# Layer norms of two expert stages move from VectorE to GpSimd, and their router is rebuilt on a padded MAX8 and a match-replace

## The reference

```
n = (t - mean(t)) / sqrt(var(t) + 1e-5)
p = softmax(n @ router)             # 8 experts
top2 values and indices of p
block 0: cw = the two values / their sum, at their experts, else 0; out = t + n + sum_e cw[e] * ffn_e(n)
block 1: cw = the two values, at their experts, else 0;             out = t + sum_e cw[e] * ffn_e(n)
```

## Time and profile before

| what | value |
|---|---|
| median of 3 runs | 6992.14 us (6990.91 to 6999.84) |
| profiled execution, own time (its span) | 6996.9 us |
| TensorE matmul / weight load busy | 5469.8 us (78%) / 4119.1 us (59%) |
| VectorE busy | 6258.5 us (89%) |
| ScalarE busy | 3507.3 us (50%) |
| GpSimd busy | 4062.8 us (58%) |
| mean granted TensorE clock | 0.748 |

### The profile page before, as it was taken

How to read it: one execution, slowest core, us unless ns; L and a number is a source line. 1 busy time by engine, 2 the same in 40 slices (tenths; PEclk the granted TensorE clock), 3 DMA queues, 4 the chain that set the end, 5 groups by cost and what they waited for, 6 DMA issues and landing times. The chain is left out here.

```text
span 6996.9 us, 144425 instructions
## 1 busy us (share of the span) xinstructions
PE 5469.8 (78%) x30242; PEld 4119.1 (59%) x30242; DVE 6258.5 (89%) x25629; ACT 3507.3 (50%) x7250; POOL 4062.8 (58%) x2812
## 2 busy tenths in 40 slices
PE   4777788887878777887878787878878787777777
PEld 2665566565656565665656565656656565656654
DVE  3999999999989999999989999998999999999941
ACT  1344455555545455555545555554545555555543
POOL 2555656565656566565656566565656566656542
PEclk9667777777777787777777777777767777777777
DMA  2111111111111111111111111111111111111100
GB/s 56 28 30 33 29 29 32 30 33 31 33 30 33 27 33 29 32 31 30 33 30 33 27 34 29 35 28 30 33 30 33 30 30 26 28 27 28 30 15 13
DMA packets 501061, 212.34 MB, mean 30 GB/s; under 512 B 339456, under 2 KB 495744, under 8 KB 500096
## 3 DMA queue, kind: packets, MB, share of 16 engines
q1 hardware_dynamic: 500096, 201.91, 12.8%
HBM read 145.29 MB, written 56.37 MB: 29 GB/s over the span
## 5 line engine op out<-in xcount | busy, mean ns | idle before, releaser
L515 POOL TENSOR_SCALAR b_r<-b_r 128x1024 f32<-128x1024 f32 x392 | 1089.2, 2778 | 1491.1 <-DVE b_r L472 1483.2
L472 DVE MATCH_REPLACE8 b_r<-b_v,b_r 128x256 f32<-128x256 f32 x4704 | 1871.2, 409 | 0.0
L467 DVE MAX8 b_v<-b_r 128x8 f32<-128x256 f32 x4704 | 1641.8, 411 | 0.0
L805 POOL TENSOR_TENSOR c_h<-c_h,c_cb 128x448 f32<-128x448 f32 x672 | 762.9, 1136 | 1083.0 <-ACT c_cb L782 1061.1
L536 PE MATMUL pT_ps<-k_ident,b_e 128*128 128x128 f32 x3136 | 644.7, 343 | 603.2 <-ACT b_pT L544 589.5
L536 PEld LDWEIGHTS pT_ps<-k_ident,b_e 128*128 128x128 f32 x3136 | 489.5, 181 | 885.7 <-issue 849.5
L438 PE MATMUL s_ps<-b_kv,b_qe 128*128 128x128 f32 x6272 | 970.5, 321 | 22.1 <-POOL b_qe L424 22.1
L438 PEld LDWEIGHTS s_ps<-b_kv,b_qe 128*128 128x128 f32 x6272 | 962.3, 242 | 22.9 <-issue 22.9
L558 PEld LDWEIGHTS o_ps<-b_kv,b_pT 128*128 128x128 f32 x6272 | 872.5, 221 | 168.8 <-issue 168.5
L558 PE MATMUL o_ps<-b_kv,b_pT 128*128 128x17 f32 x6272 | 883.8, 285 | 107.5 <-ACT b_at L585 97.5
L522 POOL TENSOR_TENSOR b_e<-b_e,b_r 128x1024 f32<-128x1024 f32 x392 | 923.3, 2355 | 38.1 <-ACT b_e L508 37.8
(11 more groups left out here) (147 smaller groups left out, 8548.8 us busy)
## 6 DMA issues: line engine op xcount, KB each, us to landing
b_kv<-kv_d SPq DMA_DIRECT2D x1568, 33.0 KB, 2.0
b_q<-q_d SPq DMA_DIRECT2D x784, 16.0 KB, 1.9
c_win<-vpad_d SPq DMA_DIRECT2D x56, 145.0 KB, 2.8
c_hm<-cpad_d SPq DMA_DIRECT2D x56, 145.0 KB, 2.3
kv_d<-a_v SPq DMA_DIRECT2D x56, 119.0 KB, 2.6
vpad_d<-a_vT SPq DMA_DIRECT2D x56, 116.0 KB, 2.3
c_win<-vpad_d SPq DMA_DIRECT2D x56, 116.0 KB, 2.7
c_row<-vpad_d SPq DMA_DIRECT2D x56, 116.0 KB, 2.5
```

The costliest lines, as they stand in the source:

```text
L467: dve.max(out=b_v8[p][:, t, 8 * rnd:8 * rnd + 8], in_=src[:, t, :]).then_inc(chain, 1)
L472: last = dve.match_replace(out=b_r[p][:, t, :], in_to_replace=b_v8[p][:, t, 8 * rnd:8 * rnd + 8], in_values=src[:, t, :], imm_value=GONE)
L515: pool.tensor_scalar(out=b_r[p][:, :, :], in0=b_r[p][:, :, :], scalar1=GONE, scalar2=None, op0=ALU.is_le).then_inc(b_msk, 1)
L805: pool.tensor_tensor(out=D["h"][g % 2][:, :], in0=D["h"][g % 2][:, :], in1=D["cb"][g % 2][:, :], op=ALU.mult).then_inc(S["hc"], 1)
```

## The change

It does the following for both c0 and c1.

- The residual add (`tok = x + pr`) moves from VectorE's step 1 to a new GpSimd step ADD, at 84.25 and 108.25. The semaphore `free` now comes from it.
- `normalise` moves from VectorE's step 2 to GpSimd's step 1, right behind `rstd`; for c0 the add `tok + xn` (`xr`) follows it there. VectorE has no step 2 any more.
- The router: ScalarE copies the 8 logits into rows of 14 whose last six columns hold 3e38 (set once, in the prologue). In VectorE's step 3 MAX8 of such a row gives the six pads and then the two largest logits (`pv`, columns 6 and 7), and MATCH_REPLACE8 writes a second copy of the row in which these eight entries are -3e38. GpSimd subtracts the largest logit from both copies (step 3), ScalarE applies Exp to both (64 columns a partition where there were 32), and GpSimd's step 4 takes the difference of the two exponentials, which is zero but for the two best experts, sums by halving adds, takes the reciprocal as a power of -1, scales, and splits the result in three bf16 parts as before. VectorE has no step 4 any more.
- `iota`, the indices, the masks and the clamp at 1e-12 (L896) are gone.
- The semaphore `x2` starts at 2 instead of 1 and its waits are one higher.

```diff
             if step == 3:
                 act.wait_ge(S["ls"], s + 2)
-                act.activation(D["p"][:, :, :], D["l"][:, :, :], ACT.Exp).then_inc(S["ex"], 1)
+                act.activation(D["p"][:, :, :, :], D["l"][:, :, :, :], ACT.Exp).then_inc(S["ex"], 1)
...
         def pool_c(pool, tau, i, step, layer):
+            if step == ADD:
+                pool.wait_ge(S["x_in"][i], LOADS[layer] * (tau + 1))
+                pool.wait_ge(S["pr"], s + 1)
...
+                pool.tensor_tensor(out=D["tok"][i][:, :, :], in0=D["x"][i][:, :, :], in1=D["pr"][:, :, :], op=ALU.add).then_inc(S["free"], 1)
             if step == 1:
                 pool.wait_ge(S["stat"], s + 1)
                 alone(pool)
                 rstd(pool, D["mv"], D["rs"], 1e-5, S["tmp"], s, S["rstd"])
-            if step == 2 and layer == 0:
-                pool.wait_ge(S["norm"], s + 1)
-                pool.tensor_tensor(out=D["xr"][i][:, :, :], in0=D["tok"][i][:, :, :], in1=D["xn"][:, :, :], op=ALU.add).then_inc(S["res"], 1)
+                pool.wait_ge(S["rstd"], s + 1)
+                alone(pool)
+                normalise(pool, D["tok"][i], D["mv"], D["rs"], D["xn"], S["sub"], s + 1, S["norm"])
+                if layer == 0:
+                    pool.wait_ge(S["norm"], s + 1)
+                    pool.tensor_tensor(out=D["xr"][i][:, :, :], in0=D["tok"][i][:, :, :], in1=D["xn"][:, :, :], op=ALU.add).then_inc(S["res"], 1)
+            if step == 3:
+                pool.wait_ge(S["top"], s + 1)
+                alone(pool)
+                pool.tensor_tensor(out=D["l"][:, :, :, :], in0=D["lr"][:, :, :, 0:NE],
+                                   in1=D["pv"][:, :, 6:7].unsqueeze(1).broadcast_to([TILE, 2, NT, NE]), op=ALU.subtract).then_inc(S["ls"], 1)
+            if step == 4:
+                pool.wait_ge(S["ex"], s + 1)
+                alone(pool)
+                pool.tensor_tensor(out=cw[:, :, :], in0=p[:, 0], in1=p[:, 1], op=ALU.subtract).then_inc(mix, 1)
+                pool.wait_ge(mix, 9 * s + 1)
+                whole = cw[:, :, :] if layer == 0 else p[:, 0]
+                pool.tensor_tensor(out=D["z4"][:, :, :], in0=whole[:, :, 0:4], in1=whole[:, :, 4:8], op=ALU.add).then_inc(mix, 1)
...
+                pool.tensor_tensor(out=D["z2"][:, :, :], in0=D["z4"][:, :, 0:2], in1=D["z4"][:, :, 2:4], op=ALU.add).then_inc(mix, 1)
...
+                pool.tensor_tensor(out=D["z"][:, :], in0=D["z2"][:, :, 0], in1=D["z2"][:, :, 1], op=ALU.add).then_inc(mix, 1)
...
+                pool.tensor_tensor(out=D["rz"][:, :], in0=D["z"][:, :], in1=k["mone"][0:TILE, 0:NT], op=ALU.pow).then_inc(mix, 1)
...
+                pool.tensor_tensor(out=cw[:, :, :], in0=cw[:, :, :], in1=D["rz"][:, :].unsqueeze(2).broadcast_to(by_expert), op=ALU.mult).then_inc(mix, 1)
...
+                pool.tensor_copy(cw3[:, :, 0, :], cw[:, :, :]).then_inc(mix, 1)
...
+                pool.tensor_tensor(out=cwd[:, :, :], in0=cw[:, :, :], in1=cw3[:, :, 0, :], op=ALU.subtract).then_inc(mix, 1)
...
+                pool.tensor_copy(cw3[:, :, 1, :], cwd[:, :, :]).then_inc(mix, 1)
...
+                pool.tensor_tensor(out=cw3[:, :, 2, :], in0=cwd[:, :, :], in1=cw3[:, :, 1, :], op=ALU.subtract).then_inc(S["cw"], 1)
...
         def dve_c(dve, tau, i, step, layer):
             if step == 1:
...
-                link(dve.tensor_tensor(out=tok[:, :, :], in0=D["x"][i][:, :, :],
-                                       in1=D["pr"][:, :, :], op=ALU.add))
-                dve.sem_inc(S["free"], 1)
+                dve.wait_ge(S["free"], s + 3)
                 mean_var(tok, mv, S["stat"])
-            if step == 2:
-                dve.wait_ge(S["rstd"], s + 1)
-                alone(dve)
-                normalise(dve, tok, mv, D["rs"], xn, S["chain"], 1, S["norm"])
             if step == 3:
                 dve.wait_ge(S["lc"], s + 1)
                 alone(dve)
-                lg = D["lg"][:, :, :]
...
-            if step == 4:
...
+                lr, pv = D["lr"], D["pv"]
                 for t in range(NT):
-                    ins = dve.max(out=D["pv"][:, t, :], in_=p[:, t, :])
+                    ins = dve.max(out=pv[:, t, :], in_=lr[:, 0, t, :])
                 link(ins)
                 for t in range(NT):
...
+                    ins = dve.match_replace(out=lr[:, 1, t, :], in_to_replace=pv[:, t, :], in_values=lr[:, 0, t, :], imm_value=GONE)
+                ins.then_inc(S["top"], 1)
```

In the lines left out of step 4, each operation waits for the semaphore of the one before it (`mix`), twice with an `alone`. The changed places:

```diff
-                 ("c0", 1): 85.7, ("c0", 2): 86.7, ("c0", 3): 88.7, ("c0", 4): 90.7, ("c0", 7): 94.7,
-                 ("c1", 1): 109.66, ("c1", 2): 111.66, ("c1", 3): 113.66, ("c1", 4): 114.66, ("c1", 7): 119.66},
-            pool={("a", 1): 4.9, ("c0", 1): 85.7, ("c0", 2): 86.7, ("c0", 7): 94.7, ("c0", 8): 96.7, ("c1", 1): 109.66},
+                 ("c0", 1): 85.7, ("c0", 3): 87.7, ("c0", 7): 94.7,
+                 ("c1", 1): 109.66, ("c1", 3): 112.66, ("c1", 7): 119.66},
+            pool={("a", 1): 4.9, ("c0", ADD): 84.25, ("c0", 1): 85.7, ("c0", 3): 88.25, ("c0", 4): 88.7, ("c0", 7): 94.7, ("c0", 8): 96.7,
+                  ("c1", ADD): 108.25, ("c1", 1): 109.66, ("c1", 3): 113.25, ("c1", 4): 113.7},
...
-                 ("c0", 0): 83.3, ("c0", TURN): 83.52, ("c0", 2): 86.68, ("c0", GATE): 87.12, ("c0", 3): 88.7,
+                 ("c0", 0): 83.3, ("c0", TURN): 83.52, ("c0", 2): 86.68, ("c0", GATE): 87.12, ("c0", 3): 88.3,
...
-                 ("c1", 0): 107.3, ("c1", TURN): 107.52, ("c1", 2): 111.7, ("c1", GATE): 112.12, ("c1", 3): 113.68,
+                 ("c1", 0): 107.3, ("c1", TURN): 107.52, ("c1", 2): 111.7, ("c1", GATE): 112.12, ("c1", 3): 113.3,
```

More of the change, by code:

```diff
@@ L221, in program @@
                 y=sem(n + "y"), yT=sem(n + "yT"), yt=sem(n + "yt", 1), stat=sem(n + "stat"),
[L222 to L224 removed]
+                tmp=sem(n + "tmp"), rstd=sem(n + "rstd"), sub=sem(n + "sub"), norm=sem(n + "norm"), res=sem(n + "res", 1),
+                xt=sem(n + "xt"), xT=sem(n + "xT"), lg=sem(n + "lg"), chain=sem(n + "chain"), top=sem(n + "top"), ls=sem(n + "ls", 1), lc=sem(n + "lc"), pr=sem(n + "pr"), tmp2=sem(n + "tmp2"),
+                ex=sem(n + "ex"), mix=sem(n + "mix"), cw=sem(n + "cw"), ct=sem(n + "ct"), cT=sem(n + "cT"),
                 h=sem(n + "h"), ge=sem(n + "ge", 2), cb=sem(n + "cb", 1), hc=sem(n + "hc"), used=sem(n + "used", 2),
[L226 removed]
+                x2=sem(n + "x2", 2), out=sem(n + "out", 16), pout=sem(n + "pout", 32)))
             cs[-1].update(stat2=sem(n + "stat2"), rstd2=sem(n + "rstd2"), norm2=sem(n + "norm2"), sub2=sem(n + "sub2"),
@@ L715, in pe_c @@
                 if g == 0:
-                    pe.wait_ge(S["x2"], s + 1)
+                    pe.wait_ge(S["x2"], s + 2)
                     alone(pe)
                     if other is not None:
-                        pe.wait_ge(O["x2"], other + 2)
+                        pe.wait_ge(O["x2"], other + 3)
                         alone(pe)
@@ L869, in dve_c @@
                 alone(dve)
-                lg = D["lg"][:, :, :]
-                link(dve.tensor_reduce(out=D["lm"][:, :], in_=lg, op=ALU.max, axis=AX.X))
-                dve.tensor_tensor(out=D["l"][:, :, :], in0=lg, in1=D["lm"][:, :].unsqueeze(2).broadcast_to(by_expert),
-                                  op=ALU.subtract).then_inc(S["ls"], 1)
-            if step == 4:
-                dve.wait_ge(S["ex"], s + 1)
-                alone(dve)
-                link(dve.tensor_reduce(out=D["z"][:, :], in_=p[:, :, :], op=ALU.add, axis=AX.X))
-                link(dve.reciprocal(D["rz"][:, :], D["z"][:, :]))
-                link(dve.tensor_tensor(out=p[:, :, :], in0=p[:, :, :], in1=D["rz"][:, :].unsqueeze(2).broadcast_to(by_expert), op=ALU.mult))
+                lr, pv = D["lr"], D["pv"]
@@ L890, in dve_c @@
-                link(ins)
-                link(dve.tensor_tensor(out=m[0][:, :, :], in0=m[0][:, :, :], in1=m[1][:, :, :], op=ALU.add))
-                ins = dve.tensor_tensor(out=cw[:, :, :], in0=m[0][:, :, :], in1=p[:, :, :], op=ALU.mult)
-                if layer == 0:
-                    link(ins)
-                    link(dve.tensor_tensor(out=D["z"][:, :], in0=D["pv"][:, :, 0], in1=D["pv"][:, :, 1], op=ALU.add))
-                    link(dve.tensor_scalar(out=D["z"][:, :], in0=D["z"][:, :], scalar1=1e-12, scalar2=None, op0=ALU.max))
-                    link(dve.reciprocal(D["rz"][:, :], D["z"][:, :]))
-                    ins = dve.tensor_tensor(out=cw[:, :, :], in0=cw[:, :, :], in1=D["rz"][:, :].unsqueeze(2).broadcast_to(by_expert), op=ALU.mult)
@@ L1029, in _ @@
                     dve.memset(d["cwT"][:, :], 0.0)
+                    dve.memset(d["lr"][:, :, :, :], -GONE)
                 for xT in xTs:
@@ L1259 @@
     lay["sel_1"] = full(np.broadcast_to((expert3[:, None, None] == expert[None, :, None]), (3 * NE, NE, 128)).astype(f))
-    lay["iota"] = np.broadcast_to(expert.astype(f), (128, NE))
     lay["mhalf"] = np.full((128, NT), -0.5, f)
+    lay["mone"] = np.full((128, NT), -1.0, f)
```

56 lines of the change are left out of this document (25 added, 31 removed).

## The result

The change made the kernel **slower**: 7135.8 us median (7130.2 to 7152.6) against 6995.2 (6990.9 to 6999.8) for the kernel before in the same series, a ratio of 1.0204 with a 95% interval of 1.0183 to 1.0225. The loss is clear of noise; whether it is a little more or a little less than 2% the runs do not tell. The time is 198 us above the forecast of 6938, inside the range, and on the other side of no change. The profiled execution spans 7150.8 us against 6996.9.

A forecast was written before the change was run, and what follows sets the result against it. VectorE was taken as a narrow bound, then TensorE's loop with ScalarE and GpSimd. 40 main strips at +0.9, 9 late at -5.8, 4 early at -12 and drain +10 gave -54 us: 6938 us median, range 6690 to 7180.

The forecast's parts named there:

- The wait of slot 0: TensorE's wait for transposed probabilities, behind VectorE's select and ScalarE's exp: relief worth 8.0 us a main strip, 11.6 late.
- The queue of slots 4 and 5: GpSimd's additions in slot 4 delay slot 5's first product: 4.0 + 1.7 + 2.7 + 1.0 us, +9.4 a main strip.
- the term of +11.5: GpSimd's queue, +9.4 us, plus +2.1 for down and values at lower clock, a main strip; bounds 6 and 14.
- The drain of +10: After 6685 us, bound by latency: the new chain is longer, +10 us.
- the 1083 us: VectorE time held by the 22 instruction groups that go, 19.3 us a strip.
- ScalarE's part in slot 1: Router Exp between two Gelus adds table loads, 2.8 us; TensorE has about 1 in hand: +1.9 us (0 to 2.8).
- Late strips: Strips after stage a is over: -11.6 - 4.5 + 1.9 + 8.4 = -5.8 us each, 9 of them.
- clock term: Without slot 0's wait, TensorE's matmuls there return to 2.4 GHz: -4.5 us a strip, main and late.
- Early strips: About 4 strips with c0 alone: c0's half of VectorE's relief, some 12 us gained each.
- The slower one: Gap moves from slot 0 to c1's first down in slot 5, no clock returned: 7281 us, clock alone 7158; chance 0.29.
- The half-hidden queue: Slots 4 and 5: half of the queue's 11.5 and 8.4 us stays hidden, 6672 us; chance 0.20.
- Nothing is won: VectorE and GpSimd: time spared on VectorE returns as longer waits between them, 6992 us; chance 0.06.

The follow-up runs named there:

- e1: Changed kernel with GpSimd's step 4 of c0 moved from slot 4 (88.7) to the end of slot 5 (89.8): 6927.2 us, ratio 0.9889.
- e3: e1 with c1's step 1 on GpSimd (rstd and norm) also moved, from 109.66 to 110.8 at the end of slot 5: 6871.6 us, 0.9809.
- x1: Changed kernel with only c1's Exp put back behind slot 1's Gelus (113.68) and GpSimd's step 4 of c1 at 114.25: 6930.1 us, 0.9902.
- n1: Kernel before with only the residual add and norms moved to GpSimd, old router kept on VectorE: 7016.2 us, 1.0043.
- r1: Changed kernel with residual add, clamp and norms back on VectorE, so the rebuilt router alone: 7021.4 us, 1.0035.
- e5: e4 with SyncE's loads of c1 moved from 106.66 in slot 1 to 105.9 at the end of slot 0: 6651.7 us, 0.9507, the best version.
- e6: e5 with VectorE's step 3 back at 88.7 and 113.66 and the router's following steps placed behind it: 6689.9 us, 0.9571.
- e7: e5 with SyncE's step 9 of c0 (writes) moved from 98.7 to 97.9, ahead of slot 0's gather: 6697.9 us, 0.9573.
- r2: r1 in e5's places, except c1's step 1 on GpSimd, which stays at 109.66: 6686.8 us, 0.9555.
- e4: e3 with both router Exps back behind their slot's Gelus (88.7, 113.68) and GpSimd's step 4 of c1 at 114.25: 6762.8 us, 0.9668.

## Why the prediction was wrong

**Right, point by point.** TensorE, ScalarE and GpSimd became the bound, and VectorE had room (75% busy, and the waits that it has for the logits). Its busy time is 154 us above the forecast's 5190, as one short product of stage b took up as much of the old stall: 363.4 us, where the same 784 instructions took 208.0 before.

```profile
L496 DVE TENSOR_TENSOR b_on<-b_o,b_rec 64x32 f32<-64x32 f32 x784 | 363.4, 464 | 185.2 <-PE o_ps L577 179.9
```

The wait of slot 0 went, and with it the lower clock of up and values, as forecast: in the main strips -11.6 us at up g2 against -12.5. GpSimd's prices held: step 4 3.95 us (4.0), its busy time 4632.7 (near 4680). The queue of slots 4 and 5 held to half a microsecond: mask to mask +8.2 on average (4.0 + 1.7 + 2.7 = 8.4), the product g6 of slot 5 moved by 2.1 + 6.8 = +8.9 against slot 3 (+9.4), and what came behind it at the lower clock +2.0 (+2.1). So the term of +11.5 measured 10.9. The sign that was named for it, 5 to 7 us of waiting for c_h once a strip, is the 5.40 us in the rows and 6.0 on average, and e1 and e3 take 264 us away by moving two items out of that slot. The drain of +10 was right, too. One count was off: the 1083 us are those of 20 groups, not 22, which changes no sum.

**The step that failed** is ScalarE's part in slot 1: "TensorE has about 1 us in hand before it needs the product: +1.9 us (0 to 2.8)". It measured 11.6 - 7.1 = **+4.5 us** a main strip, and x1, which undoes it alone, gives 5.0 us of such a strip back. Two things were missed. I looked at the product, but behind the Exp and its loads in ScalarE's list also stands b_at, which the values need and for which TensorE already waited 0.65 us at that place in the kernel before. There was no slack, and the 2.86 us count in full: the wait went from 0.7 to 3.8 us, means of the main strips. And the wait that this makes lets TensorE fall to 1.2 GHz, so that the values take 3.4 us for 2.0 on average. I gave that price to the gap of slot 5 and not to the gap that I made in slot 1. With 4.5 for 1.9 a main strip comes to 0.9 + 2.6 = 3.5; +0.9 from slot 0, +0.3 in slots 2 and 3 and -0.6 from the queue make it the 4.1 measured. This one term is enough to turn the sign: with 4.5 us in 40 main strips and the 6.7 of slot 1 in 9 late ones (see below) the sum comes to 6938 + 40 x 2.6 + 9 x 4.8 = 7085 us.

**Late strips** came out at -0.1 for -5.8, and here two terms failed (means of nine strips). Slot 0 gave 8.9 us at up g2 for the forecast's 16.1. Its clock term was nearly void: the values of slot 0 took 2.1 us already before the change. And part of its wait only moved on: in slot 1 the transposes wait 3.2 us for ScalarE's copy of the probabilities, where they waited 0.9. Slot 1 cost 6.7 us for 1.9. x1 gives about half of that back; the moved wait stays in x1 (3.4 us). The queue cost 3.8 us for 8.4, which hides part of both errors.

**Early strips**: the four with c0 alone gained 24.6 us in all (-1.3, -9.5, -6.1, -7.7) for the forecast's 48, and the fifth distance, in which c1 begins, lost 7.0. My 12 us each rested on VectorE's relief, not on a wait of TensorE in that stretch.

The errors add up: +125 in the main strips, +51 late, +30 early, 2 in the prologue, 208 us of the profiled execution.

**The rivals.** The slower one (chance 0.29) put its place in slot 5, with no clock given back. Its direction came true and its mechanism in part. The clock of slot 0 came back in the main strips, and the queue cost 10.9 us and not the upper bound of 14. But it was right that the gaps only move and TensorE runs at 1.2 GHz behind them, in slots 1, 4 and 5: TensorE's busy time rose by 157 us, and the mean granted clock fell from 0.748 to 0.739. The half-hidden queue is refuted, since the queue counted in full. "Nothing is won" is refuted by e1: the same operations on the same engines are 1.1% faster with one step placed elsewhere. Here the Trainium skill ("Perfetto Trace Analysis", Optimizing Scalar/DVE Operations), which doubts moves between VectorE and GpSimd for their shared read port, is half borne out: 155 us of stall did come back on VectorE's short product, but on an engine with room, and the loss has other causes. In e1 the same product is busy for 639.4 us, 276 more than in the changed kernel, and e1 is the faster one by 209 us. Where VectorE was still the busiest engine, in n1, the stall took back all of the relief.

**Why the halves do not add.** r1 and n1 both lose little, together 2.0%. The trace of r1 gives TensorE 280.1 us of waiting for c_h against 363.4: each half alone lengthens the queue of slot 4 by about what its gain elsewhere pays for; the second half adds its 1.7 us norm (mask to mask 24.5 us in r1, 26.2 with both) to a queue that is already the last to arrive, while the select it relieves is no longer waited for. That reading fits the waits, but no run tested it by itself.

**What the prediction left out, and what bounds the best version.** It looked at SyncE only for new transfers. SyncE's own time of about 115 us a main strip never bound the changed kernel (124.7), but it is why e5 gained less than its wait promised and why e5, e6, e7 and r2 all stand at 115 to 116 us. In e4 (117.1) it waited only 12.7 us of 1000. This is read from its waits; no run made its queue shorter. The late strips, where SyncE does pause, are at 103 to 104 us in these four runs, and what bounds them stays open.

## What to carry to other kernels

When work moves to an in-order queue, list everything that stands behind the insertion point, not just the consumer that you have in mind, and ask of each whether TensorE already waits for it by a few tenths; if so, the insertion counts in full and the matmuls behind it may fall to the lower clock on top. A side engine's average (GpSimd 65% here) says nothing about the slot in which a strip's last link lies. The move was worth 4.9% once its steps were placed after the products that TensorE waits for: place first, then judge the move. (No run gave the kernel before the earlier load of e5; its convolution waited for that load only 22.4 us in all.) And ask of the engine that issues the transfers what is asked of every other: how long it is at work a strip. When a wait for a load does not shrink though the load is moved forward, read that engine's own waits.
